# Two-layer attention, gated FFN and selective scan on 8 cores: weight loads of the h1 and h2 loops issued by ScalarE, ternarize buffers allocated from the right end of SBUF

## What is computed

```python
xn = layernorm(x)
q, k, v = (einsum('bsm,hmd->bhsd', xn, kernel[i]) for i in range(3))      # 16 heads of 64
s = einsum(softmax(q @ k.T * scale) @ v, WO)                              # layer 0 mixer
h = silu(xn @ w1.T * w1_s) * (xn @ w2.T * w2_s)                           # [4096 x 4096 hidden]
h = gelu(h @ h1.T * h1_s)                                                 # h1: 4096 x 4096
h = gelu(h @ h2.T * h2_s)                                                 # h2: 4096 x 4096
g = silu(h @ w3.T * w3_s)
x = x + s * g
xn = layernorm(x)
s = selective_scan_block(xn)                                              # layer 1 mixer, 16 states
g = silu(layernorm(gelu(xn @ absmean(W_fc).T)) @ absmean(W_proj).T)       # absmean: weights to -1, 0, 1
x = x + s * g
```

## Time and profile before

| | us |
|---|---|
| median of 13 runs | 18566.27 |
| lowest, highest | 18280.75, 19020.33 |
| the profiled execution | 18280.75 |
| its span on the slowest core | 18279.2 |
| spans of all cores | 18139.3 to 18279.2 |

### The profile page before, as it was taken

The page is one execution under the profiler, slowest core; times in us unless marked ns, Lnnn a source line. Parts: engine busy times, 40 slices in busy tenths (PEclk is TensorE's granted clock), DMA queues, the critical chain, the costliest instruction groups (busy, mean ns, idle before and its releaser), DMA issues.

```text
span 18279.2 us, 120178 instructions; the slowest of 8 cores (18139.3 to 18279.2 us)
## 1 busy us (share of the span) xinstructions
PE 10388.9 (57%) x39884; PEld 3857.1 (21%) x39884; DVE 5036.6 (28%) x7592; ACT 5014.3 (27%) x6161; POOL 112.5 (1%) x215
## 2 busy tenths in 40 slices
PE   0000568879688797796877968851333233332457
PEld 0000222324223232242332423320100010000123
DVE  0032010000000000000000000003788898888821
ACT  0000134161340521614416144111332233222300
POOL 0001000000000000000000000000000000000000
PEclk9999778989889887898988988975555555555578
DMA  9953432323223232242332422331111101110032
GB/s 115 117 135 117 91 65 95 127 68 137 89 91 132 73 109 96 68 150 79 101 121 69 141 81 100 124 94 54 35 35 35 32 20 37 35 35 27 25 109 91
DMA packets 743263, 1533.44 MB, mean 84 GB/s; under 512 B 302498, under 2 KB 425507, under 8 KB 657460
## 3 DMA queue, kind: packets, MB, share of 16 engines
q1 hardware_dynamic: 715540, 1334.90, 23.1%
q0 software_dynamic: 27120, 190.85, 6.7%
HBM read 1396.88 MB, written 292.18 MB: 92 GB/s over the span
## 4 chain that ended last, share of the span: by engine, by line
PE 37%; DVE 22%; ACT 12%; SPq 10%; DMA 9%; issue 9%; DVEq 1%; POOL 0%; ACTq 0%; POOLq 0%
PE pl L1030 10%; PE pl L1057 10%; SPq L125 8%; ACT c_at L883 8%; DVE s_ht L1509 7%; DVE s_bu L1503 4%; DVE s_cht L1524 3%; PE pl L1091 3%; PE pl L970 2%; DMA c_q<-q_scr 2%; SPq L123 2%; PE pl L980 1%; PE pl L603 1%; PE pl L1722 1%; PE pl L1726 1%
## 5 line engine op out<-in xcount | busy, mean ns | idle before, releaser
L883 ACT ACTIVATE c_at<-pl,c_cpool 128x1024 f16<-128x1024 f32 x2048 | 2081.5, 1190 | 206.4 <-PE pl L875 204.9
L1030 PE MATMUL pl<-d_hin,d_whb 128*128 128x512 bf16 x8192 | 1826.5, 387 | 95.9 <-DMA d_whb<-h1m 95.9
L1057 PE MATMUL pl<-d_hmid,d_whb 128*128 128x512 bf16 x8192 | 1816.4, 386 | 9.9 <-ACT d_hmid L1043 8.3
L1111 DVE TENSOR_TENSOR d_g<-pl,d_w3sbc 128x512 f32<-128x512 f32 x64 | 41.0, 683 | 4467.1 <-PE pl L1091 4467.1
L1569 PE MATMUL pl<-f_hh,c_onescol 128*1 128x512 bf16 x256 | 127.3, 497 | 2007.9 <-ACT f_hh L1562 2007.9
L1509 DVE TENSOR_TENSOR_SCAN s_ht<-s_at,s_st,s_bu 128x512 f32<-128x512 f32 x896 | 1149.9, 1283 | 97.1 <-DVE s_bu L1503 4.6
L1498 ACT ACTIVATE s_at<-s_dl,s_A 128x512 f32<-128x512 f32 x1024 | 705.6, 717 | 1615.0 <-DVE s_ht L1509 1574.9
L869 PE MATMUL pl<-c_q,c_k 64*128 64x512 bf16 x2048 | 795.7, 394 | 489.7 <-DMA c_q<-q_scr 250.1
L1030 PEld LDWEIGHTS pl<-d_hin,d_whb 128*128 128x128 bf16 x8192 | 813.6, 99 | 1108.8 <-issue 257.1
L1057 PEld LDWEIGHTS pl<-d_hmid,d_whb 128*128 128x128 bf16 x8192 | 811.5, 99 | 1014.8 <-issue 168.9
L1551 PE MATMUL pl<-f_xnf,f_wfb 128*128 128x512 bf16 x2048 | 872.8, 604 | 30.1 <-DMA f_wfb<-wfc16m 30.1
(11 more groups left out here) (189 smaller groups left out, 9972.7 us busy)
## 6 DMA issues: line engine op xcount, KB each, us to landing
d_whb<-h1m SPq DMA_DIRECT2D x256, 1024.0 KB, 5.4
d_whb<-h2m SPq DMA_DIRECT2D x256, 1024.0 KB, 4.9
c_v<-v_scr SPq DMA_DIRECT2D x64, 1040.0 KB, 8.5
c_k<-k_scr SPq DMA_DIRECT2D x64, 1024.0 KB, 5.5
d_w1b<-w1m SPq DMA_DIRECT2D x256, 256.0 KB, 3.2
d_w2b<-w2m SPq DMA_DIRECT2D x256, 256.0 KB, 3.5
d_w<-w3T SPq DMA_DIRECT2D x256, 256.0 KB, 4.5
f_wfb<-wfc16m SPq DMA_DIRECT2D x256, 256.0 KB, 2.6
```

The source lines that it names most:

```text
L883: e.activation(attAB[tb % NAP][:, :], self.pl[r][:, :], AF.Exp, scale=self.cp(2)),
L1030: r = e.matmul(self.pb[bank][:, :], whb[j][:, kb * 128:(kb + 1) * 128], hin[kb][:, :], start=(kb == 0), stop=(kb == HB - 1))
L1057: r = e.matmul(self.pb[bank][:, :], whb[j][:, kb * 128:(kb + 1) * 128], hmid[kb][:, :], start=(kb == 0), stop=(kb == HB - 1))
```

## The change

Three things change. The DMAs that load `whb` in the loops h1 and h2 are issued by ScalarE in place of SyncE, at the same place in the program. The ternarize tiles are allocated from the right end of SBUF, and the loads of phase B no longer wait for `tz_sbuf_done`. Phase D, whose tiles reach to the right end, waits for it instead, at its first scale load and at the first loads of `xnf`, k and v. The barrier is not changed.

```diff
-            def sbuf(self, name, shape, dt):
-                return st.enter_context(kern.nc.sbuf_tensor(name, shape, dt))
+            def sbuf(self, name, shape, dt, side=None):
+                return st.enter_context(
+                    kern.nc.sbuf_tensor(name, shape, dt, side=side))
...
                     tok = p.dma("sync", f"b_w{j}", wsb[j][kb][:, :],
                                 self.d[name16][kb * 128:(kb + 1) * 128, :],
-                                waits=list(waits)
-                                + getattr(self, "tz_sbuf_done", []))
+                                waits=list(waits))
...
-                            waits=[xnf_consumed]
-                            + getattr(self, "tz_sbuf_done", []),
-                            transpose=True)
+                            waits=[xnf_consumed], transpose=True)
...
-                blk = [sc.sbuf(f"tz_b{j}", [128, KB * 128], F32)
-                       for j in range(2)]
-                outb = [sc.sbuf(f"tz_o{j}", [128, KB * 128], BF16)
-                        for j in range(2)]
+                blk = [sc.sbuf(f"tz_b{j}", [128, KB * 128], F32,
+                               side="right") for j in range(2)]
+                outb = [sc.sbuf(f"tz_o{j}", [128, KB * 128], BF16,
+                                side="right") for j in range(2)]
...
-                t_scl = p.dma("sync", "d_scl", scl[nm][:, :], self.d[nm])
+                t_scl = p.dma("sync", "d_scl", scl[nm][:, :], self.d[nm],
+                              waits=getattr(self, "tz_sbuf_done", []))
...
                                self.d["k_scr"][hp * 128:(hp + 1) * 128, :],
-                               waits=[kcons[0]])
+                               waits=[kcons[0]]
+                               + (getattr(self, "tz_sbuf_done", [])
+                                  if c == 0 and hp == 0 else []))
...
-                    tlh = p.dma("sync", f"d_whl{j}", whb[j][:, :],
+                    tlh = p.dma("scalar", f"d_whl{j}", whb[j][:, :],
                                 self.d["h1m16"][m], waits=[whl_tok[j],
                                                            self.wwait("h1")])
...
-                    tlh = p.dma("sync", f"d_whl{j}", whb[j][:, :],
+                    tlh = p.dma("scalar", f"d_whl{j}", whb[j][:, :],
                                 self.d["h2m16"][m], waits=[whl_tok[j],
                                                            self.wwait("h2")])
```

More of the change, by code:

```diff
@@ L847, in phase_D @@
                                                  i * 128:(i + 1) * 128],
-                                waits=[xnf_cons], transpose=True)
+                                waits=[xnf_cons]
+                                + (getattr(self, "tz_sbuf_done", [])
+                                   if c == 0 else []),
+                                transpose=True)
                 for hp in range(NHEAD // 2):
@@ L859, in phase_D @@
                     tv = p.dma("sync", "c_vld", vpb[0][:, :],
-                               self.d["v_scr"][hp], waits=[vcons[0]])
+                               self.d["v_scr"][hp],
+                               waits=[vcons[0]]
+                               + (getattr(self, "tz_sbuf_done", [])
+                                  if c == 0 and hp == 0 else []))
                     def emit_scores(tb):
```

## The result

| | us |
|---|---|
| median of 11 runs after | 21654.93 (21563.63 to 21699.29) |
| ratio to the kernel before, both measured side by side | 1.178, 95% interval 1.174 to 1.182 |
| span of the profiled execution, slowest core (3) | 21677.1 |
| spans of all its cores | 21516.4 to 21677.1 |

The changed kernel is slower by 18%. The forecast was 22,200 in a range of 21,300 to 23,300. From profile to profile the slowest core's span grew by 21677.1 - 18279.2 = 3398 us, where the sum had 3775. The code moved down by 7 lines: h1 is now line 1037 (gelu 1050), h2 line 1064 (gelu 1078), w3 line 1098. In some executions one die's four cores show a lower granted clock than the other's, so the spans and stretches of the experiments are those of cores of the die with the higher clock in the profiled execution ("the faster die").

The account below looks back on a forecast made before the run. h1 and h2 were taken to run at TensorE's own pace, loads hidden. Exposed loads 3931 - 8 - 52 - 2 - 94 = 3775 us on 18,281 gave 22,056, plus half of 285: 22,200 us, range 21,300 to 23,300.

Parts of the forecast that it names:

- The order on ScalarE: In h1 and h2, load(m+1) goes out only when block m is finished: 504 exposed loads, 3931 us with clock loss.
- the rival in which the issue isn't held: ScalarE's queue between gelus: a load passes a waiting gelu and stays hidden; about 18,230 us, or 18,510; 3%.
- The price of a stop: h1 and h2, block end to next first matmul: release, issue, landing, start and drain sum to 5.7 us (5.05 to 6.8).
- Release and issue: ScalarE starts 0.09 us after the matmuls; the load issues 0.4 us later, halfway between bounds 0.05 and 0.75.
- The clock: Blocks of h1 and h2 start slowly after each stop: 2.1 us lost, making one step 7.8 us.
- doesn't fall: Rival: stops of 5.5 us in h1 and h2 are too short to lower the clock; 21,140 us; 6%.
- stays down for whole blocks: Rival: h1 and h2 blocks run at half clock throughout, 6.9 us more each; 24,620 us; 6%.
- The ends of the loops: h1's first load goes out earlier, its stop shrinks by 5 to 8 us; 52 us gained over 8 chunks.
- The slow chunk: One h1 plus h2 stretch at clock 0.82 lost 94 us; with TensorE idling, that loss was taken as gone.
- The half of 285 us: The median of 13 runs before lay 285 us above the profiled execution; half was added to the sum, giving 22,200 us.
- Ternarize: Phase A's barrier still waits for ternarize, so the moved waits save only 2 us at line 121.
- B moves under ternarize: Rival: phase B starts under ternarize, saving up to 450 + 252 us of SyncE's barrier wait; 21,500 us; 2%.

Follow-up runs that it names:

- second and third experiment: Second: changed kernel with h1 and h2 loads still on ScalarE, load m+1 listed ahead of gelu m; 18,001 to 18,027 us on the faster die. Third: own line.
- half-load kernel: Changed kernel loading only 512 KB of each h1 and h2 weight block, the very first two excepted, other half stale; 21,598 us in one execution.
- third experiment: Changed kernel with h1 and h2 loads issued by SyncE, each held back until the block before is done; 1.184 times the kernel before.

## Why the prediction was right, and where its sizes were off

**The order on ScalarE** (load(m+1) behind gelu(m), 504 exposed loads): right in every row, and shown from both sides by the second and third experiment; the rival in which the issue isn't held is out. The forecast said 2800 us of stops; it is 2663.9.

**The price of a stop**, by its terms. Release and issue: 0.09 + 0.4 were taken; the chain shows gelu's start 0.08 us after the matmuls and the load 0.02 after that. The lower bound of the issue, 0.05, was the true one, and halfway cost 0.38 x 504 = 192 us. Landing: 4.8 taken; 4.9 to 5.0 in the steps of the chain, 4.8 as the median of the run. Landing to matmul: 0.2 taken, 0.25 measured. Without the drain the sum had 5.49; the page shows 5.20 (core 3), and core 6 below 5.18.

**The clock.** Its size is best read on a core of the faster die, core 6 (groups of instructions, after):

```profile
L1037 PE MATMUL pl<-d_hin,d_whb 128*128 128x512 bf16 x8192 | 2191.3, 435 | 1324.2 <-DMA d_whb<-h1m 1324.2
L1064 PE MATMUL pl<-d_hmid,d_whb 128*128 128x512 bf16 x8192 | 2185.5, 434 | 1327.8 <-DMA d_whb<-h2m 1327.8
```

A block takes (2191.3 + 2185.5)/512 = 8.55 us. The drain is in it, so drain and clock together, 8.55 - 6.91 = 1.64, stand against 0.17 + 2.1 = 2.27. Filling the stops gave back 1.57. The step that was off most is the choice of 2.1 in the middle of 1.35 and 2.9, read from bursts elsewhere: 0.63 x 504 = 318 us too much. Both rival clocks are out: "doesn't fall", since filling gained 766 us, and "stays down for whole blocks", which needed 6.9 us a block where 1.6 were measured.

**One step in all**: 7.8 forecast; 5.18 + 8.55 - 6.91 = 6.82 measured. 504 x 6.82 - 8 - 52 = 3377 us, beside 3386 measured in phase D (core 6 against core 4 before): the count and the sum's form hold.

**The ends of the loops**: the stop at h1's head shrank from 11.75 to 4.95, by 6.8 us where 5 to 8 were forecast.

**The slow chunk**: 94 us were taken as gone, because TensorE would idle for a third of the time. That reason failed. On the slowest core after, one h1 loop runs at clock 0.74 (the stretch from 9403.40 above), with blocks of up to 10.85 us, and phase D is 12,771.8 us there, 119 more than on core 6. Before, the slowest core's phase D (core 1, 9381.9 us) was 115 more than core 4's. So the loss stayed, in loops with stops as well. This error has the other sign and hid a part of the first: (7.8 - 6.82) x 504 - 94 = 400 us, and the forecast's sum was 3775 - 3398 = 377 too large. That the two partly cancel is luck.

**The half of 285 us** that was added for the median of before was not borne out: after's runs lie within 136 us of each other, and their median is 22 below the span of the profiled execution. So the forecast was 545 us too high: 377 by the sum, 143 by this half, and 22 by that.

**Ternarize**: right. The barrier waits stayed, the 2.1 us went, and putting SyncE back left nothing of the change to be seen. The rival "B moves under ternarize" holds only once the barrier counts otherwise.

## What to carry to other kernels

A double buffer is worth only as much as the place of its load in the list of the engine that issues it: the load must stand ahead of everything there that waits for the work which should hide it. Before a load is moved to another engine, write down that engine's list as it will read, and before a wait is moved, look whether a barrier repeats it. The price of an exposed load is its landing plus the clock that the stop costs. In the one run with shorter stops the second part did not shrink with the first but grew.

## What the runs showed of the hardware that was not expected

- A load in ScalarE's list behind an activation goes out 0.01 to 0.07 us after the activation starts, while it still runs for 0.69 us.
- In the half-load kernel, stops of 3.8 us came with more loss of clock than stops of 5.2 in after: blocks of 9.74 us against 8.55, so that a step of 13.73 us became one of 13.54 only. This is one execution, with stale weights; its cause stays open. With dummy matmuls in the stop, after's loads gave a stretch at clock 1.00, and the kernel that did more work on TensorE was faster by 766 us in phase D. The Trainium skill describes a loop whose bursts start slowly again after each wait for a DMA ("TensorE: Matmul & The Clock Gate", section "HAM oscillation — how this bites in real kernels"); the rows of after agree with it, at 440 ns for a matmul where the earlier trace rows had 387.
- After's runs differ less from each other than those of before: 136 us from lowest to highest, against 740 in the 13 runs shown of before. It is not shown that the stops do this: the third experiment has the same stops, and its runs spread over 323 us.
